# Layer 1's edge features: two tiles transposed as one square, and target one-hots compared on VectorE

## The reference

```
h = relu(layernorm(x));  x = x + L0(h)
h = relu(layernorm(x));  x = x + L1(h)

L0: deg = segment_sum(1, dst) + 1;  dis = rsqrt(deg);  g = h @ W
    out = segment_sum(g[src] * dis[src] * dis[dst], dst) + g * dis^2 + b
    return h + gelu(out)

L1: m   = concat(h[src], h[dst], edge_attr) @ msg_W1 + msg_b1      # 192 -> 64
    msg = relu(m) @ msg_W2 + msg_b2
    agg = segment_sum(msg, dst)
    return relu(concat(agg, h) @ upd_W1 + upd_b1) @ upd_W2 + upd_b2
```

## Time and profile before

| | |
|---|---|
| median of 3 runs | 2382.3 us |
| the runs | 2382.29, 2382.3, 2398.0 us |
| the profiled execution | 2395.71 us |
| its span in the profile | 2393.9 us |
| mean granted clock of TensorE in it | 0.938 of full speed |
| layer 1's loop over the edges | from about 893 to 2354 us of the span |

### The profile page before, as it was taken

The page is one execution under the profiler, slowest core; times in us unless marked ns, Lnnn a source line. Parts: engine busy times, 40 slices in busy tenths (PEclk is TensorE's granted clock), DMA queues, the critical chain, the costliest instruction groups (busy, mean ns, idle before and its releaser), DMA issues.

```text
span 2393.9 us, 72611 instructions
## 1 busy us (share of the span) xinstructions
PE 2169.2 (91%) x23690; PEld 1951.6 (82%) x23690; DVE 1706.6 (71%) x4619; ACT 1143.6 (48%) x2411; POOL 1600.1 (67%) x1574
## 2 busy tenths in 40 slices
PE   2255999999999569999999999999999999999998
PEld 1143888887888458999999999999999999999995
DVE  8866888887888766666666666666666666666662
ACT  0004888888888433444444444444444444444442
POOL 5375777777775115777777777777777777777771
PEclk7566999999999758999999999999999999999999
DMA  2002111111111022333333333333333333333332
GB/s 73 1 1 44 26 27 28 27 28 28 27 27 19 4 68 59 74 73 73 76 75 74 73 73 73 73 73 76 74 74 74 75 73 75 76 74 73 73 74 36
DMA packets 345718, 133.10 MB, mean 56 GB/s; under 512 B 304301, under 2 KB 321555, under 8 KB 345587
## 3 DMA queue, kind: packets, MB, share of 16 engines
q1 hardware_dynamic: 297780, 82.40, 15.2%
q0 software_dynamic: 47808, 49.05, 11.3%
HBM read 123.78 MB, written 7.52 MB: 55 GB/s over the span
## 4 chain that ended last, share of the span: by engine, by line
PE 87%; DVE 7%; issue 3%; POOL 2%; DMA 1%; ACT 1%; SPq 0%; DVEq 0%; PEld 0%; PEldq 0%; POOLq 0%; ACTq 0%
PE psum L1737 17%; PE psum L1679 14%; PE psum L1548 12%; PE psum L1751 12%; PE psum L1580 9%; PE psum L1670 8%; PE psum L1689 5%; PE psum L1569 2%; PE psum L1715 2%; POOL rows L665 1%; PE psum L1704 1%; PE psum L1559 1%; PE psum L1640 1%; PE psum L1515 1%; DVE work L813 1%
## 5 line engine op out<-in xcount | busy, mean ns | idle before, releaser
L665 POOL DMA_INDIRECT rows<-a_rows,idx x1078 | 1049.8, 974 | 449.9 <-issue 306.0
L1319 ACT ACTIVATE hT<-psum 128x392 bf16<-128x392 f32 x1152 | 510.7, 501 | 101.6 <-PE psum L1580 93.4
L665 POOL DMA_INDIRECT rows<-g_rows,idx x416 | 431.4, 1037 | 145.8 <-issue 126.7
L1548 PE MATMUL psum<-work,hT 128*128 128x192 bf16 x3528 | 455.5, 247 | 0.3 <-ACT hT L1319 0.3
L1737 PE MATMUL psum<-edge_index,H 128*128 128x192 bf16 x4802 | 429.9, 247 | 2.4 <-DVE H L1092 2.4
L1372 ACT ACTIVATE eoT<-psum 128x512 f32<-128x512 f32 x392 | 213.8, 602 | 409.3 <-PE psum L1670 409.3
L1737 PEld LDWEIGHTS psum<-edge_index,H 128*128 128x128 bf16 x4802 | 398.9, 99 | 4.0 <-DVE H L1092 2.5
L1548 PEld LDWEIGHTS psum<-work,hT 128*128 128x128 bf16 x3528 | 324.0, 99 | 71.0 <-issue 1.4
L1580 PE MATMUL psum<-Z,one_lo 128*128 128x392 f16 x1152 | 365.5, 339 | 15.6 <-DVE Z L929 15.4
L1679 PE MATMUL psum<-wb,eoT 128*128 128x64 f32 x3136 | 376.0, 273 | 0.0
L1679 PEld LDWEIGHTS psum<-wb,eoT 128*128 128x128 f32 x3136 | 367.3, 193 | 0.1
(11 more groups left out here) (272 smaller groups left out, 2060.2 us busy)
## 6 DMA issues: line engine op xcount, KB each, us to landing
work<-in_edge_attr_dram SPq DMA_DIRECT2D x390, 128.0 KB
rows<-a_rows,idx POOLq DMA_INDIRECT x1078
Z<-slot_code SPq DMA_DIRECT2D x98, 160.0 KB
rows<-g_rows,idx POOLq DMA_INDIRECT x416
idx<-src_by_tile SPq DMA_DIRECT2D x199, 4.0 KB
wb<-b_rows SPq DMA_DIRECT2D x196, 16.0 KB, 2.0
g_rows<-Y SPq DMA_DIRECT2D x1, 1600.0 KB, 8.9
a_rows<-Y SPq DMA_DIRECT2D x6, 256.0 KB, 2.6
```

Of the source, the lines that this page charges most:

```text
L665: pool.indirect_dma_start(out=rows[:, k, t, :], out_offset=None, in_=table, in_offset=bass.IndirectOffsetOnAxis(ap=idx[:, k, t:t + 1], axis=0)
L1319: nc.scalar.activation(counts[:, j % 2, :, t * SLOTS:(t + 1) * SLOTS], psum[:, t % 4, 0:KEYS].rearrange("p (h m) -> p h m", m=SLOTS), ACT.Copy
L1548: ins = TT.matmul(psum[:, 4 + (j + 1) % 2, 0:NPART * D], counts[:, (j + 1) % 2, h, :], gtab[:, h, :, :].rearrange("p k d -> p (k d)"), sta ...
```

## The change

Edge features and one-hots no longer share a square. `edges` holds the features alone, so two tiles' features (2 x 64 columns) stand side by side and are transposed as one square: 4 transposes per superblock instead of 8. After it the even tile's features lie on partitions 0 to 63 and the odd tile's on 64 to 127. ACT copies them to those partitions of `eoT`, even and odd tiles apart. The other half of each tile in `eoT`, the transposed one-hots, is no longer transposed: the target numbers of the superblock (int32) are sent by DMA to 64 partitions each, and DVE compares them with base + lane (`mark_targets`, two instructions of 64 partitions x 512 numbers per superblock). Since the halves lie the other way round for odd tiles, a second weight tile `wb_odd` has the target rows above the edge weights, and PE does the even tiles' terms first, then the odd ones'. The untransposed one-hots for the sums stay, now in `to_node`. DVE does `mark_targets` for superblock n+2 straight behind `add_rows` of n. `transpose_edges` waits for the loads alone and for the copies of two superblocks before; `sum_messages` takes the wait for the one-hots. SP loads the indices ahead of the wait for the sums, then edge features (2 DMAs), targets (2, for k = 3 three), and both weight tiles' target rows.

```diff
+        edges, to_node = (work[:, q * U * T * D:(q + 1) * U * T * D].rearrange("p (u t d) -> p u t d", u=U, t=T) for q in range(2))
...
             def load_superblock(r, s, k, tiles, rest):
-                sp.wait_ge(summed[1], r * NSB + s + 1)
...
                 if k != KPE:
                     sp.wait_ge(added, r * NSB + s + 1)
                     sp.dma_start(idx[:, k, :], src_dram[:, bass.ds(s * T, T)]).then_inc(idx_in[1][k], 16)
+                sp.wait_ge(summed[1], r * NSB + s + 1)
+                parts = LOADS[k] - 3
+                if rest is None:
+                    for half in range(2):
+                        sp.dma_start(edges[:, k, half * 4:half * 4 + 4, :],
+                                     edge_x[bass.ds(s * SB + half * 4 * P, 4 * P), :].rearrange("(t p) d -> p t d", p=P)
+                                     ).then_inc(e_in[k], 16)
+                    to = dst[bass.ds(s * SB, SB)].rearrange("(a j q e) -> q a j e", a=1, q=2, e=P)
+                    sp.dma_start(targets[k][0:W, :].rearrange("p (j e) -> p j e", e=P), wide(to[1], 0, W)).then_inc(e_in[k], 16)
+                    for c in range(parts):
+                        j = slice(c * T // 2 // parts, (c + 1) * T // 2 // parts)
+                        sp.dma_start(targets[k][W:2 * W, :].rearrange("p (j e) -> p j e", e=P)[:, j, :], wide(to[0, :, j, :], 0, W)
+                                     ).then_inc(e_in[k], 16)
...
+                sp.dma_start(wb[D:2 * D, k, :], b_dram[bass.ds(b0, W), :]).then_inc(b_in[k], 16)
+                sp.dma_start(wb_odd[0:D, k, :], b_dram[bass.ds(b0, W), :]).then_inc(b_in[k], 16)
...
+                V.tensor_scalar(pass_tmp[:, :], base[:, :], lane[:, :], None, ALU.add)
...
+                    def mark_targets(i, k, older=True):
+                        dve.wait_ge(e_in[k], LOADS[k] * 16 * (r * NIT + i + 1))
+                        if older:
+                            dve.wait_ge(pre_done, r * NSB + i * U + k - 1)
+                        for h in range(2):
+                            half = slice((1 - h) * D, (2 - h) * D)
+                            V.tensor_scalar(eoT[half, k % 2, h::2, :], targets[k][half, :].rearrange("p (j e) -> p j e", e=P),
+                                            pass_tmp[half, bass.ds(i * U + k, 1)], None, ALU.is_equal).then_inc(target_marked, 1)
...
                         add_rows(i, k)
+                        if not last or k + 2 < U:
+                            mark_targets(*ahead(i, k, 2))
                         if k % 2 == 0:
...
+                    for k in range(2):
+                        mark_targets(0, k, False)
                     edges_to_slots(0, 0, first=True)
...
-                        nc.scalar.activation(eoT[:, k % 2, h * 4:h * 4 + 4, :],
-                                             psum[:, h, :].rearrange("p (t e) -> p t e", e=P), ACT.Copy).then_inc(eoT_ready, 1)
+                        half = slice(h * D, (h + 1) * D)
+                        nc.scalar.activation(eoT[half, k % 2, h::2, :], psum[half, k % 2, :].rearrange("p (j e) -> p j e", e=P),
+                                             ACT.Copy).then_inc(eoT_ready, 1)
...
-                    pe.wait_ge(onehot[1], n + 1)
-                    pe.wait_ge(e_in[k], 32 * (r * NIT + i + 1))
...
+                    pe.wait_ge(e_in[k], LOADS[k] * 16 * (r * NIT + i + 1))
+                    if not first:
+                        pe.wait_ge(eoT_ready, 2 * n - 2)
+                    for j in range(T // 2):
+                        ins = TT.transpose(psum[:, k % 2, j * P:(j + 1) * P],
+                                           edges[:, k, 2 * j:2 * j + 2, :].rearrange("p t d -> p (t d)"), ident[:, :])
+                    ins.then_inc(transposed, 1)
...
+                    pe.wait_ge(b_in[k], 32 * (r * NIT + i + 1))
+                    for h, weights in enumerate((wb, wb_odd)):
+                        pe.wait_ge(target_marked, 2 * n + 1 + h)
+                        pe.wait_ge(eoT_ready, 2 * n + 1 + h)
+                        for t in range(h, T, 2):
+                            ins = TT.matmul(psum[:, 2 + k % 2, t * D:(t + 1) * D], eoT[:, k % 2, t, :], weights[:, k, :],
+                                            start=True, stop=True)
```

More of the change, by code:

```diff
@@ L89, in gnn_two_layers @@
     NCODE = -(-NPT // P)
+    LOADS = (4, 4, 4, 5)
     NRANK = -(-BINS * NPT // 512)
@@ L191, in gnn_two_layers @@
         gtab = work[:, :].bitcast(bf16).rearrange("p (h k d) -> p h k d", k=NPART, d=D)
-        eo = work[:, 0:U * T * 2 * D].rearrange("p (u t d) -> p u t d", u=U, t=T)
+        edges, to_node = (work[:, q * U * T * D:(q + 1) * U * T * D].rearrange("p (u t d) -> p u t d", u=U, t=T) for q in range(2))
         wb = sb("wb", [P, U, D])
@@ L214, in gnn_two_layers @@
         slot = sb("slot", [P, 1])
+        lane_i = sb("lane_i", [P, 1], i32)
+        lane = sb("lane", [P, 1])
         slot_node = sb("slot_node", [P, CH * T])
@@ L251, in gnn_two_layers @@
         picked_rows = y_flat[:, o:o + BINS * NPART * D // 2].bitcast(bf16).rearrange("p (b c) -> p b c", b=BINS)
+        o += BINS * NPART * D // 2
+        hist_lo, hist_hi = (t[:, :, :, :].rearrange("p a m t -> p (a m t)").bitcast(f32) for t in (one_lo, one_hi))
+        HALF = SB // 2
+        targets = [b[:, q * HALF:(q + 1) * HALF].bitcast(i32) for b in (hist_lo, y_flat[:, o:o + 2 * HALF]) for q in range(2)]
+        wb_odd = hist_hi[:, 0:U * D].rearrange("p (u d) -> p u d", u=U)
         from_slot = z_flat[:, 0:BINS * GE // 2].bitcast(bf16).rearrange("p (b e) -> p b e", b=BINS)
@@ L495, in _ @@
                                  held[:, c * T:c * T + m, :]).then_inc(stored, 16)
+            for k in range(U):
+                sp.dma_start(wb_odd[D:2 * D, k, :], msg_w1[2 * D:3 * D, :]).then_inc(s_wc, 16)
             sp.wait_ge(s_ad, 16 * NCHUNK)
@@ L511, in load_superblock @@
             def load_superblock(r, s, k, tiles, rest):
-                sp.wait_ge(summed[1], r * NSB + s + 1)
-                if rest is None:
-                    for half in range(2):
-                        sp.dma_start(eo[:, k, half * 4:half * 4 + 4, 0:D],
-                                     edge_x[bass.ds(s * SB + half * 4 * P, 4 * P), :].rearrange("(t p) d -> p t d", p=P)
-                                     ).then_inc(e_in[k], 16)
-                else:
-                    sp.dma_start(eo[:, k, 0:tiles, 0:D],
-                                 edge_x[s * SB:s * SB + tiles * P, :].rearrange("(t p) d -> p t d", p=P)).then_inc(e_in[k], 16)
-                    sp.dma_start(eo[0:rest, k, tiles, 0:D], edge_x[s * SB + tiles * P:E, :]).then_inc(e_in[k], 16)
-                b0 = sp.value_load(base_i[0:1, bass.ds(s, 1)], min_val=0, max_val=NP - W)
-                sp.dma_start(wb[D:2 * D, k, :], b_dram[bass.ds(b0, W), :]).then_inc(b_in[k], 16)
                 if k != KPE:
@@ L526, in load_superblock @@
                     sp.dma_start(idx[:, k, :], src_dram[:, bass.ds(s * T, T)]).then_inc(idx_in[1][k], 16)
+                sp.wait_ge(summed[1], r * NSB + s + 1)
[11 more added lines that the diff above has]
+                                     ).then_inc(e_in[k], 16)
+                else:
+                    e0 = s * SB
+                    sp.dma_start(edges[:, k, 0:tiles, :],
+                                 edge_x[e0:e0 + tiles * P, :].rearrange("(t p) d -> p t d", p=P)).then_inc(e_in[k], 16)
+                    sp.dma_start(edges[0:rest, k, tiles, :], edge_x[e0 + tiles * P:E, :]).then_inc(e_in[k], 16)
+                    for rows_, first, n, at in ((slice(0, W), P, P, 0), (slice(W, 2 * W), 0, P, 0), (slice(W, 2 * W), 2 * P, rest, P)):
+                        sp.dma_start(targets[k][rows_, at:at + n],
+                                     wide(dst[e0 + first:e0 + first + n].rearrange("(a e) -> a e", a=1), 0, W)).then_inc(e_in[k], 16)
+                b0 = sp.value_load(base_i[0:1, bass.ds(s, 1)], min_val=0, max_val=NP - W)
+                sp.dma_start(wb[D:2 * D, k, :], b_dram[bass.ds(b0, W), :]).then_inc(b_in[k], 16)
+                sp.dma_start(wb_odd[0:D, k, :], b_dram[bass.ds(b0, W), :]).then_inc(b_in[k], 16)
             with sp.Fori(0, passes1) as r:
@@ L546, in _ @@
                     else:
+                        assert left // P == 2 and left % P and k == U - 1
                         load_superblock(r, s, k, left // P, left % P)
@@ L1306, in _ @@
             nc.scalar.activation(w_out[:, :], w_upd2[:, :], ACT.Copy, scale=0.5).then_inc(s_wTc, 1)
-            act.wait_ge(s_codeT, 1)
+            act.wait_ge(s_wT, 3)
             nc.scalar.activation(code_rows[:, 0:NCODE - 1, :], psum[:, 5, 0:(NCODE - 1) * P].rearrange("p (a e) -> p a e", e=P),
@@ L1688, in sum_messages @@
                         half = (t % 2) * D
-                        ins = TT.matmul(psum[half:half + D, 4, 0:W], msg[:, k % 2, t, :], eo[:, k, t, D:2 * D],
+                        ins = TT.matmul(psum[half:half + D, 4, 0:W], msg[:, k % 2, t, :], to_node[:, k, t, :],
```

38 lines of the change are left out of this document (14 added, 24 removed).

## The result

The change makes the kernel slower: 2566.26 us (four runs, 2555.59 to 2569.63) against 2389.95 us for the kernel before (four runs), a ratio of 1.073, 95% interval 1.0688 to 1.0772. That is +176 us, where +56 was forecast. The profiled execution took 2567.64 us, with a span of 2565.8.

What follows compares the result with a forecast made beforehand. The prediction took a ring through PE and DVE to bound the kernel: +53 us for the ring and +3 for the start made +56, or 2438 us against the median of 2382.3. Its 8-in-10 range was 2405 to 2490.

Steps and rivals of the forecast that it cites:

- The ring: Odd step's sums, DVE's even step, packing, PE's odd step, sums: 14.71 us a pair, to grow by 0.55, +53 us.
- DVE's wait for returned rows: Before DVE's third reduction in the even step; 0.22 us a pair, expected to vanish as the ring's only gain.
- transposes: On PE, 1.08 us each superblock; half of them was to take 0.54, or 1.08 saved per pair.
- that rival: PE was the bound after all, ranks don't hold packing: 64 us faster, 2318; 12 in 100.
- The odd step's slack on DVE: DVE's 2.95 us of idle before its addition of sums; covers the odd step's compares, leaving about 2.2 us.
- the three signs that the prediction named for being wrong: Packing starting without following the ranks, compares lasting 0.6 us or more, or PE's waits naming a DMA.
- The compares' length: On DVE behind the rows' addition: 467 ns each, moving what follows by 0.77 us per pair of compares; bounds 0.63 and 1.22.
- The start: First loads, issued ahead of the edge load's release, and marking of two superblocks before the first ranks: 3 us, bounds 1 and 6.
- The clock: A clock falling with PE's new waits would cost more on top; given no case of its own.
- It has room: POOL's 22 gathers need 28.1 us in four superblocks, of 29.4 before the change and 30.5 after.
- a rival: POOL held up by DVE's two-port mode: eight compares hold gathers 3.1 us, 34 us more, 2472; 5 in 100.

Runs made afterwards that it cites:

- loads-only kernel: The kernel before with the changed kernel's loads, except the index load's place, into the same tiles, read by nobody; ratio 1.0032.
- The fill: The changed kernel with PE doing the odd step's four transposes four times over before it waits for the ranks; 2562.44 us.
- compares-only kernel: The kernel before with the two compares per superblock on numbers in SBUF, into a tile that nobody reads; ratio 1.0729.
- fewer-gathers kernel: The changed kernel with POOL leaving out two gathered tiles of each superblock that has any, 16 in four superblocks instead of 22; 2532.29 us.

## Why the prediction was wrong

**The ring: right.** Packing follows the ranks by 0.22 us as before, PE waits 1.71 us a pair where about 1.7 was forecast, DVE's wait for returned rows is gone, transposes take 110.4 us in 175 superblocks, 0.63 each for 0.54, so half the transposes did not take half the time. PE's idle time is 12% for 11. PE was never the bound, and that rival falls. The odd step's slack on DVE is 2.3 us in pairs that nothing disturbs (2.2 forecast). None of the three signs that the prediction named for being wrong appeared, though the time lay far outside: they watched the ring, and what failed lay beside it.

**The compares' length: too small.** 467 ns was forecast and 496 measured, but the pair of them moves what follows by 1.04 us and not 0.77: from L1154's start to L1126's 1516.15 - 1514.51 = 1.64, where the earlier trace rows had 0.60. Of this 0.12 stands ahead of the first compare, which starts 0.72 us behind L1154 and not 0.60, and 0.92 are the two compares. The ring's pairs take 15.45 us (38 undisturbed ones) against 14.71, +0.74 for +0.55 forecast: 97 x 0.74 = 72 us instead of 53.

**The start: at its upper bound.** 6 us for 3, by the loads, as the loads-only kernel shows.

**The clock: a case that the prediction saw and gave no chance.** The step that failed reads "I give that no case of its own". The stretch's 1.00 came from an engine that hardly waited, and the forecast itself gave it 1.7 us of waiting per pair. In the changed kernel 50 of 96 pairs are 1.6 us longer than the ring, 79 us. The fill shows that it is the wait: PE's work in its place takes away all 50 falls at packing. What picks the 50 is open: the waits before them are 1.5 to 1.9 us, 1.73 on average, and those of the other pairs 1.65. With the ring's 72 and the start's 6 this leaves 15 us of the profiled 172 for the six pairs with waits for gathered rows.

**POOL: "It has room" failed, and with it the price of a rival.** The rule of the Trainium skill ("SBUF — State Buffer", "SBUF: two separate sides") was put at 5 in 100 and 2472, since a gather beside L1092 grew by only 0.15. The runs say that gathers grow by 0.22 on average, 4.8 us in 22, over the 3.1 that I worked out as the rule's worst: POOL needs 22 x 1.497 = 32.9 us in four superblocks and not 28.1, more than the 30.5 that the ring was to leave it. The compares' own length is the wrong measure: of the 212 us by which the 863 gathers from 1000 to 2300 us exceed 0.944 each (the time of one that meets nothing on DVE), only 16 are in the 229 that meet a compare and not the run of seven behind it (L1135), and 119 are in the 85 that meet this run. POOL and DVE of the changed kernel, side by side:

```profile
1507.05 1.03 DVE L1091 TENSOR_SCALAR eoT<-one_lo,pass_tmp 64x512 f32<-64x512 int32 x2
...
1507.62 2.42 POOL L687 DMA_INDIRECT rows<-a_rows,idx  x1 [0.30 <-issue]
1508.08 2.14 DVE L1135 TENSOR_SCALAR Z<-Z,slot_cmp 128x640 bf16<-128x640 f16 x7
```

and the same seven instructions in the loads-only kernel, DVE's row and then POOL's:

```profile
1511.79 2.34 DVE L1119 TENSOR_SCALAR Z<-Z,slot_cmp 128x640 bf16<-128x640 f16 x7 [0.26 <-DMA Z<-slot_code]
```

```profile
1512.15 0.95 POOL L683 DMA_INDIRECT rows<-a_rows,idx  x1 [0.31 <-issue]
1513.40 0.95 POOL L683 DMA_INDIRECT rows<-a_rows,idx  x1 [0.30 <-issue]
```

Without the compares the gathers pass through this run untouched, and DVE needs 2.34 us. With them one gather lasts as long as almost the whole run, 2.42 us, and DVE needs 2.14. From 1400 to 1700 us 19 gathers of the changed kernel meet this run; they take 2.30 us on average, 26 of the 52 us by which the 199 gathers there exceed 0.944. In the compares-only kernel it is the same, 19 at 2.29. In the kernel before, some 62 meet it at 0.95. So an old instruction that cost POOL nothing began to cost it 1.4 us, because of what now stands before it. The rule agrees with the sign. A hold over seven instructions, where it speaks of one, and that the same run lets gathers pass at other times are not in it. With the compares ahead of it, gathers that start 0.45 us before the run or 0.07 after its start are held (2.42 and 2.60), and one that starts 0.6 after is not (0.95); in the kernel before, ones that start 0.36 to 0.5 us before the run pass as well, so the start alone doesn't decide. What does, I can't say.

**Why +176, and not one of its parts.** Two limits of nearly the same height lie over the ring: the clock's, 16.24 us a pair when POOL is out of the way, and POOL's, 16.5 when no clock falls at packing. The ring needs 15.45. In the changed kernel both are there: it has the clock's pairs and six with gather waits, and POOL, which waits 32.3 us for indices in 1450, hardly rests. That is why removing either brought 34 us or nothing. Why the two come so close is not known; POOL's need is no constant, since a gather's length depends on what it meets on DVE. That both removed together leave the ring at 15.4 was not seen: the kernel for it ran only on the chips with gaps on PE. What stands in its place is weaker, the pairs that neither disturbs: 15.42 to 15.54 us in three kernels, with 8 or 11 gathers a pair and with or without fill.

## What to carry to other kernels

Before moving work to an engine with idle time, follow the ring: from the wait that ends that idle time back to itself. Busy shares showed 31% of DVE free, but in the half of the pair that mattered it idled only in its own issue and 0.16 us besides. When a removal leaves an engine waiting more, ask what its clock does then, and count the next limit with prices taken after the change, not before: here both the clock and the gathers got worse from the same edit. And when removing a proven cause gives nothing, look for a second limit of the same height before dropping the cause.

## What the runs showed of the hardware

- PE, waiting 1.5 to 1.9 us before packing once in 15 to 17 us and otherwise busy, ran on at a granted clock of 0.58 over the next 4 us in about half of the cases (50 and 47 of 96), then at 1.00. Waits of the same length stood before the other half. With waits of 0.42 us on average at this place it never did; what was left there, 23 falls, came behind waits for gathered rows.
- The same seven DVE instructions let gathers pass (0.95 us each) or held one for 2.42 us, in the same kernel too (85 that met them in the changed kernel took 2.34 us on average, most 2.4 to 2.6 and a few 0.95). They took 2.14 us when they held one and 2.3 when two or three passed; in the fewer-gathers kernel also 2.14 when they met none (21 times).
- Gathers that met two-source compares (64x512, int32 and f32 in SBUF) and not the run behind them took 0.98 us on average, where an undisturbed one takes 0.944; in the same run, gathers beside the seven took up to 2.28.
- The same chip ran the kernel before in 3917 and, 34 minutes later, in 2396 us. Other kernels, profiled in the slow time, show gaps of a microsecond and more between matmuls on PE that nothing in the profile explains.
